# Flamingo layer with routed experts: block tables built with one block per partition, and four pieces of the attention turns in another order

## The reference

```python
# x (8, 256, 256), ctx (8, 120, 256)
qh, kh, vh = x_norm @ Wq, ctx @ Wk, ctx @ Wv   # 16 query heads in 4 groups, 4 key heads of 16
attn = softmax(rope(sum of groups of qh) . rope(kh) / 4)
x = x + tanh(g_xattn) * ((attn @ vh).mean over heads @ Wo)
# experts: 2048 tokens, 8 experts, top 2
probs = softmax(layernorm(x) @ gate_w.T);  w, idx = top_k(probs, 2);  w = w / sum(w)
for e in range(8):
    g, u = split(layernorm(x) @ gate_up_proj[e].T)
    acc += combine[:, e] * (silu(g) * u @ down_proj[e].T)
x = x + tanh(g_ffn) * acc
```

## Time and profile before

| | us |
|---|---|
| median of 3 runs | 457.68 |
| lowest and highest | 455.27, 459.23 |
| the profiled execution | 455.51 |
| its span, first to last instruction | 453.7 |

### The profile page before, as it was taken

The page is one execution under the profiler, slowest core; times in us unless marked ns, Lnnn a source line. Parts: engine busy times, 40 slices in busy tenths (PEclk is TensorE's granted clock), DMA queues, the critical chain, the costliest instruction groups (busy, mean ns, idle before and its releaser), DMA issues.

```text
span 453.7 us, 10877 instructions
## 1 busy us (share of the span) xinstructions
PE 407.9 (90%) x2468; PEld 342.4 (75%) x2469; DVE 220.6 (49%) x589; ACT 204.9 (45%) x453; POOL 258.3 (57%) x257
## 2 busy tenths in 40 slices
PE   7877787666799999999999999999999999999960
PEld 6644464444688888888898888988889888888850
DVE  2566998886334434344443344443444434434330
ACT  2569866221563246336435622563347336433210
POOL 3116879853467239936953972498229936953221
PEclk9999888859699999999999999999999999999975
DMA  8960024821054213531632461146213541112110
GB/s 274 404 249 25 23 97 169 275 73 48 1 175 138 51 24 110 160 102 24 209 117 42 137 192 24 24 116 210 46 24 89 162 122 24 24 24 37 37 28 12
DMA packets 19625, 46.68 MB, mean 103 GB/s; under 512 B 2369, under 2 KB 13761, under 8 KB 16513
## 3 DMA queue, kind: packets, MB, share of 16 engines
q1 hardware_dynamic: 11632, 35.20, 22.4%
q0 software_dynamic: 6720, 9.64, 11.6%
q10 hardware_dynamic: 1248, 1.57, 1.0%
HBM read 37.67 MB, written 9.00 MB: 103 GB/s over the span
## 4 chain that ended last, share of the span: by engine, by line
PE 75%; DVE 9%; DMA 4%; ACT 3%; POOL 3%; issue 3%; POOLq 1%; SPq 0%; DVEq 0%; ACTq 0%
PE att L1010 21%; PE sc L990 20%; PE misc L990 10%; PE qbank L990 10%; PE pT L1000 6%; DMA x<-in_x 2%; POOL dn L472 2%; PE att L974 2%; ACT gu L638 1%; PE att L789 1%; DVE stats L1074 1%; PE sc L827 1%; DMA out<-xT_all,index_out 1%; DVE dn L1201 1%; PE qbank L814 1%
## 5 line engine op out<-in xcount | busy, mean ns | idle before, releaser
L530 POOL DMA_INDIRECT out<-xT_all,index_out x34 | 54.5, 1604 | 111.8 <-DVE xT_all L1421 97.2
L1010 PE MATMUL att<-dn,hT 128*128 x816 | 115.8, 292 | 0.6 <-DVE hT L1399 0.6
L1010 PEld LDWEIGHTS att<-dn,hT 128*128 128x128 f32 x816 | 103.0, 192 | 1.0 <-issue 0.9
L990 PE MATMUL sc<-gu,xT 128*128 x408 | 102.4, 400 | 0.0
L990 PEld LDWEIGHTS sc<-gu,xT 128*128 128x128 f32 x408 | 74.1, 188 | 14.7
L990 PE MATMUL misc<-gu,xT 128*128 x204 | 81.5, 400 | 1.5 <-ACT xT L711 0.9
L990 PE MATMUL qbank<-gu,xT 128*128 x204 | 81.6, 400 | 0.0
L397 POOL TENSOR_TENSOR gu<-wraw,gu 128x2048 f32 x14 | 64.4, 4614 | 12.8 <-ACT gu L627 12.0
L1395 DVE TENSOR_TENSOR xT_all<-xT_all,sc 128x512 f32<-128x512 f32 x34 | 23.4, 688 | 87.6 <-ACT xT_all L718 87.6
L718 ACT ACTIVATE xT_all<-misc 128x512 f32<-128x512 f32 x34 | 20.3, 598 | 81.0 <-PE qbank L990 74.8
L1395 DVE TENSOR_TENSOR xT_all<-xT_all,qbank 128x512 f32<-128x512 f32 x34 | 23.4, 688 | 62.7 <-ACT xT_all L718 62.7
(11 more groups left out here) (169 smaller groups left out, 482.8 us busy)
## 6 DMA issues: line engine op xcount, KB each, us to landing
wraw<-in_gu SPq DMA_DIRECT2D x16, 1024.0 KB, 5.4
wraw<-in_dn SPq DMA_DIRECT2D x8, 1024.0 KB, 5.2
x<-in_x SPq DMA_DIRECT2D x8, 266.0 KB, 11.7
xT_all<-in_xT SPq DMA_DIRECT2D x4, 512.0 KB, 11.3
out<-x SPq DMA_DIRECT2D x8, 256.0 KB, 2.2
rows_scratch<-x SPq DMA_DIRECT2D x3, 532.0 KB, 3.9
xT_all<-rows_scratch,index_in POOLq DMA_INDIRECT x37, 2.9
out<-xT_all,index_out POOLq DMA_INDIRECT x34, 3.9
```

Of the source, the lines that this page charges most:

```text
L530: nc.gpsimd.indirect_dma_start(out=out_d, out_offset=bass.IndirectOffsetOnAxis(ap=index, axis=0), in_=y[:, r, :], in_offset=None, compute_ ...
L990: mm = nc.tensor.matmul(bank[2 * hf + n][:, :], xT[:, par, xp, k, :], gu_part(where, wp, k * 2 * I + col, HALF), start=(k == 0 and xp == 0 ...
L1010: mm = nc.tensor.matmul(bank[6][:, 0:D], hT[:, hf, hp, j * P:(j + 1) * P], dn_part(where, wp, (hf * JH + j) * D, D), start=(hf == 0 and j ...
```

## The change

**The tables.** Block s now stands on partition s. Two columns of constants, `row` (the partition's number) and `row_above` (one less), take the place of the row `blocks`. Fifteen operations of 8 elements a partition (the sum has 32) make five columns `tab_rows`; PE multiplies each column with the identity, which lays the five out as 5 x 44 numbers on partition 0 of the bank `misc`; one DVE copy writes `tab`. There is one semaphore for all readers, `tables_ready`, and POOL's second to sixth gathers and PE's step 0 wait for it. `aside` is a helper for an operation that nothing right behind it needs. PE now warms with one matmul ahead of the five small ones and one behind them.

```diff
             pe.wait_ge(pT_copied, TB * B)
-            stay_warm(3)
+            stay_warm(1)
+            pe.wait_ge(rows_tabled, 1)
+            for k in range(5):
+                mm = nc.tensor.matmul(tab_ps[:, k * NCOL:(k + 1) * NCOL], tab_rows[:, k:k + 1], ident[:, 0:NCOL],
+                                      start=True, stop=True)
+            mm.then_inc(tab_psum, 1)
+            stay_warm(1)
             transpose_x(0)
-            pe.wait_ge(experts_ready, 1)
+            pe.wait_ge(tables_ready, 1)
             step(0, 0, first=True)
```

```diff
             find_tokens()
-            link(V.tensor_tensor(by_block, for_blocks(endblk[:, :]), all_blocks, ALU.is_le))
-            link(V.tensor_reduce(tabf[:, 0, :], by_block, AX.X, ALU.add))
...
+            aside(V.tensor_scalar(by_row[:, 0, :], endblk[:, :], c("row"), None, ALU.is_le))
+            aside(V.scalar_tensor_tensor(out=by_row[:, 1, :], in0=endblk[:, :], scalar=c("row"), in1=skip[:, :],
+                                         op0=ALU.is_le, op1=ALU.mult))
...
+            link(V.tensor_reduce(row_sum[:, :], by_row[:, :, :], AX.X, ALU.add))
...
+            dve.sem_inc(rows_tabled, 1)
+            dve.wait_ge(tab_psum, 1)
+            V.tensor_copy(tab[0:1, :, :], tab_ps.rearrange("o (k s) -> o k s", k=5)).then_inc(tables_ready, 1)
             x_low(0, 0)
-            link(V.tensor_tensor(by_base, by_block, for_blocks(skip[:, :]), ALU.mult))
...
-            V.tensor_tensor(tab[:, 2, :], tabf[:, 1, :], tabf[:, 2, :], ALU.add).then_inc(tables_ready, 1)
```

```diff
-                elif t + 3 < B:
-                    first_moments(t + 3)
-                if ranked is not None:
-                    for b in SETS[ranked]:
-                        mark_slots(b)
                 if t >= 1:
                     best_two(t - 1)
...
+                if ranked is not None:
+                    for b in SETS[ranked]:
+                        mark_slots(b)
                 if t >= 1:
                     second_moments(t - 1)
+                    if t + 3 < B:
+                        first_moments(t + 3)
```

```diff
                 if t < B:
                     copy_pT(t, 0)
-                if t - 2 in ENDS:
-                    second_odds(ENDS[t - 2])
...
                 if t + 1 < B:
                     exponentials(t + 1, 0)
                     exponentials(t + 1, 1)
+                if t - 2 in ENDS:
+                    second_odds(ENDS[t - 2])
```

```diff
                 elif t - 2 in ENDS:
-                    share_out(ENDS[t - 2])
                     place_values(ENDS[t - 2])
                     for b in SETS[ENDS[t - 2]]:
                         mark_places(b, PICKS)
+                    share_out(ENDS[t - 2])
```

More of the change, by code:

```diff
@@ L86, in _const_columns @@
     for name, n in (("ident", P), ("kcos", A), ("ksin", A), ("rope", S), ("before", P), ("prio", E),
-                    ("base", E), ("limits", E * NT), ("upto_it", E * E), ("blocks", NCOL),
+                    ("base", E), ("limits", E * NT), ("upto_it", E * E), ("row", 1), ("row_above", 1),
                     ("first", E), ("alone", E), ("second", E), ("place", P), ("begin", BEGINS), ("token", NT),
@@ L206, in build_program @@
         assert at + (DEPTH - 1) * PICKS * P <= 2 * DN
-        at = E * NT + 2 * NCOL * E
-        at += 2 * NCOL * E
+        at = E * NT
         from_begin = area[:, at:at + BEGINS]
-        assert at + BEGINS <= KC * B * A and PICKS * P <= 2 * NCOL * E
+        assert at + BEGINS <= KC * B * A
         late = xT_all[:, :, :].rearrange("p k n -> p (k n)")
@@ L1357, in _ @@
-            link(V.tensor_tensor(first_by[:, :, :], first_by[:, :, :], over(skip[:, :], FIRSTS), ALU.mult))
-            link(V.tensor_reduce(first_f[:, :], first_by[:, :, :], AX.X, ALU.add))
-            V.tensor_tensor(first_tab[:, :], first_f[:, :], c("blocks")[:, 0:FIRSTS], ALU.add).then_inc(firsts_ready, 1)
-            link(V.tensor_tensor(by_block, for_blocks(endblk[:, :]), all_blocks, ALU.is_le))
-            link(V.tensor_reduce(tabf[:, 0, :], by_block, AX.X, ALU.add))
-            link(V.tensor_scalar(tab[:, 0, :], tabf[:, 0, :], float(E - 1), None, ALU.min))
@@ L1377, in _ @@
-            link(V.scalar_tensor_tensor(out=piece_code[:, 0, :], in0=nblk[:, :], scalar=1.0, in1=c("alone"),
-                                        op0=ALU.is_equal, op1=ALU.mult))
-            link(V.tensor_tensor(piece_code[:, 0, :], piece_code[:, 0, :], c("first"), ALU.add))
-            link(V.tensor_copy(piece_code[:, 1, :], c("second")))
-            for n in range(2):
-                link(V.tensor_tensor(by_piece[:, n, :, :], for_blocks(piece_at[:, n, :]), all_blocks, ALU.is_equal))
-                link(V.tensor_tensor(by_piece[:, n, :, :], by_piece[:, n, :, :], for_blocks(piece_code[:, n, :]),
-                                     ALU.mult))
@@ new lines, in _ @@
+            aside(V.scalar_tensor_tensor(out=by_row[:, 1, :], in0=endblk[:, :], scalar=c("row"), in1=skip[:, :],
+                                         op0=ALU.is_le, op1=ALU.mult))
+            aside(V.tensor_tensor(startblk[:, :], endblk[:, :], nblk[:, :], ALU.subtract))
+            aside(V.scalar_tensor_tensor(out=code_second[:, :], in0=nblk[:, :], scalar=1.0, in1=c("second"),
+                                         op0=ALU.is_gt, op1=ALU.mult))
+            link(V.scalar_tensor_tensor(out=code_first[:, :], in0=nblk[:, :], scalar=1.0, in1=c("alone"),
+                                        op0=ALU.is_equal, op1=ALU.mult))
@@ new lines, in _ @@
+            aside(V.tensor_scalar(tab_rows[:, 3:4], endblk[:, E - 1:E], c("row"), None, ALU.is_gt))
+            aside(V.scalar_tensor_tensor(out=by_row[:, 3, :], in0=startblk[:, :], scalar=c("row_above"), in1=code_second[:, :],
+                                         op0=ALU.is_equal, op1=ALU.mult))
+            link(V.tensor_tensor(code_first[:, :], code_first[:, :], c("first"), ALU.add))
+            link(V.scalar_tensor_tensor(out=by_row[:, 2, :], in0=startblk[:, :], scalar=c("row"), in1=code_first[:, :],
+                                        op0=ALU.is_equal, op1=ALU.mult))
@@ new lines, in _ @@
+            link(V.tensor_reduce(row_sum[:, :], by_row[:, :, :], AX.X, ALU.add))
+            aside(V.tensor_scalar(tab_rows[:, 0:1], row_sum[:, 0:1], float(E - 1), None, ALU.min))
+            aside(V.scalar_tensor_tensor(out=tab_rows[:, 4:5], in0=row_sum[:, 1:2], scalar=c("row"), in1=tab_rows[:, 3:4],
+                                         op0=ALU.add, op1=ALU.mult))
+            aside(V.tensor_copy(tab_rows[:, 1:2], row_sum[:, 3:4]))
+            aside(V.tensor_scalar(last_block[:, :], endblk[:, E - 1:E], -1.0, None, ALU.add))
@@ L1477, in shape_constants @@
     put("upto_it", (np.arange(E)[None, :] <= np.arange(E)[:, None]).reshape(1, E * E))
-    put("blocks", np.arange(NCOL)[None, :])
+    put("row", np.arange(P)[:, None])
+    put("row_above", np.arange(P)[:, None] - 1)
     put("place", np.arange(P)[None, :])
```

59 lines of the change are left out of this document (17 added, 42 removed).

## The result

| | before | after |
|---|---|---|
| median | 456.21 us | 453.48 us |
| lowest, highest of 20 runs | 453.19, 459.29 | 451.12, 455.77 |
| the profiled execution | 455.51 us | 451.98 us |
| its span | 453.7 us | 450.2 us |

What follows compares the result with a forecast made beforehand. PE was taken to bound the expert blocks, so gains lay ahead of the loop and in PE's clock. 455.51 - 2.7 (wait) - 2.65 + 2.4 (clock) + 0.75 (turns) = 453.3 profiled, median 455.5; range 451.5 to 460.

Steps and rivals of the forecast that it cites:

- The wait: PE ahead of the loop: the idle 2.41 us goes, plus 0.3 of the next 0.61; gain 2.7 us.
- The second gather: POOL's second gather waits for the whole table; its stage comes near 108.4, covered by 1 us, so no cost.
- The clock behind the idle time: Loop's first matmuls and the transposes no longer run at the low clock behind PE's idle stretch; gain 2.65 us.
- The clock in step 0: With less warming, step 0's first twelve matmuls run at the low clock; cost 2.4 us, bounds 0 and 4.8.
- The turns: Reordered work in the turns: 1.25 us lost in turn 7, 0.5 won in turn 5; 0.75 us later in sum.
- Turn 5: DVE's comparisons move mostly out of the time of POOL's splits; 0.5 us won, between 1.9 won and 0.9 lost.
- The slower rival: Turns 3, 5 and 7 plus low clock lose more than the tables win; 4.0 us slower, 461.7; chance 0.12.
- signs of being right: No ACT table wait, no PE idle over 1 us before the loop, tables' copy near 104, first group 5 us.
- sign of being wrong: token_at later than 102.5 or sooner than 99.5, a stage-bound second transpose, full clock throughout step 0, or new low loop stretch.

Runs made afterwards that it cites:

- warm_two: The changed kernel with two warming matmuls instead of one ahead of the wait for the table columns; 452.23 us, ratio 0.9897 to before.
- tables_warm2: New tables, turns as before, two warming matmuls instead of one ahead of the columns; 451.71 us, ratio 0.9876 to before; repeated: 450.67 us, 0.9880.
- tables_moments_odds: New tables, turns as before except first_moments at the end of a turn and second_odds behind the exponentials; 452.99 us, ratio 0.9908 to before.
- turns_only: The kernel before with only the four edits in the turns, old tables kept; 457.69 us, ratio 1.0025 to before.
- tables_marks_late: New tables, turns as before except mark_slots moved behind the choice and the logit gap; 452.47 us, ratio 0.9897 to before.
- after_again: The changed kernel itself, unmodified, timed once more beside other variants; 453.85 us, ratio 0.9925 to before.
- tables_only: The changed kernel with its four edits in the turns undone; 451.32 us, ratio 0.9893 to before; repeated: 451.78 us, 0.9920.

## Why the prediction was right, and where it was not

The medians differ by 2.7 us where I had 2.2, and the two profiled executions by 3.5. The mechanism of the tables and of the clock held; that of the turns did not, though its sum came out near. Term by term:

**The wait.** The step held, its size was a little too small. From the start of step 0 to the loop the four traces with full clock there (`warm_two`, `tables_warm2`, its repetition and `tables_moments_odds`) take 6.19 to 6.69 us; before took 9.79, with full clock up to its idle stretch. That is 3.1 to 3.6, where I had 2.7. Of the missing part 0.3 is in the 0.61 us of idle time ahead of the loop's first matmul, of which I took half, as the entry to the loop. It was all wait: PE now has no idle time there, so the wait was 2.41 + 0.61 = 3.0. The rest is the transposes ahead of it, 0.78 us at the low clock and 0.60 now; they start 0.35 us ahead of the loop's first matmul (115.12 to 115.47), where it was 1.39. I had put 0.25 for them under the clock. The tables came in 3.35 us behind `token_at`, against my 3.8, and ACT waits for no table:

```profile
ACT xT_all L706 <- PE qbank L978: 1.9, 1, 1.9
```

This single wait stands in place of the 6.2 us of the earlier trace rows, and it is for PE. The five small matmuls took 0.89 at the low clock; I had 1.1, and up to 2.2.

**The second gather.** Forecast near 108.4, found at 109.81: the tables came 0.7 us later than forecast, behind the later `token_at`, and between them and POOL's copy lie 1.0 us where I had 0.2. It still cost nothing in this trace, since PE transposes these rows behind the first half, which the low clock had made longer. In `tables_warm2`, where that half was at full clock, PE waited 0.32 us for this stage. The cover of 1 us was used up.

**The clock behind the idle time.** 2.65 forecast. The loop's first step takes 12.29 us before and 9.56 to 9.58 in all twelve traces with the new tables: 2.7 less. Right. (From the loop to the end it is 337.24 against 334.45 to 335.40, 1.8 to 2.8 less; there the end of the kernel adds its own spread.)

**The clock in step 0.** 2.4 forecast for a first half that is all low, bounds 0 and 4.8. The change paid 7.71 - 6.25 = 1.5 in one trace and 2.5 in the other; of the eight traces with one warming matmul one had the full clock by itself (`tables_moments_odds`, 6.19), the seven others paid 1.5 to 2.5. All three traces with two matmuls there and none further ahead had it full. So with one matmul 1 trace of 8 and with two 3 of 3 have the full clock from step 0's start. The mechanism is shown in kind; which of its ends an execution meets varies. I had quoted the Trainium skill's page "TensorE: Matmul & The Clock Gate" ("Part 1: The HAM clock gate") for a place of the transition that varies from run to run, with no row to bear it out; the two traces of one program, 7.71 and 8.72, now do.

**The turns.** The sum of 0.75 lies near the 1.1 us of `turns_only` [-0.4, 2.6], but its reason was wrong, and so this part of the forecast was right by luck. I wrote that in turn 7 nothing takes the place of the comparisons, and charged 1.25 us for DVE. The idle time came (1.70 us, as forecast), and yet in the trace of after it isn't what ends last. DVE and POOL in turns 7 and 8:

```profile
83.63 0.25 DVE L1132 MAX8 top<-att 128x8 f32<-128x8 f32 x2 [1.70 <-PE att L856]
...
86.71 1.37 DVE L1195 TENSOR_TENSOR dn<-const,slot_f 128x552 fp32r<-128x552 f32 x2
...
93.61 0.16 DVE L1220 SCALAR_TENSOR_TENSOR x<-mv,x 128x2 f32<-128x2 f32 x1 [1.29 <-POOL x L409]
93.69 0.73 DVE L1195 TENSOR_TENSOR dn<-const,slot_f 128x552 fp32r<-128x552 f32 x1
...
97.02 0.16 DVE L1220 SCALAR_TENSOR_TENSOR x<-mv,x 128x2 f32<-128x2 f32 x1 [0.70 <-POOL x L409]
```
```profile
84.39 7.42 POOL L467 TENSOR_SCALAR dn<-const,slot_f,value 128x128 fp32r<-128x128 f32 x8
91.78 0.29 POOL L445 TENSOR_TENSOR route<-route,odds 128x64 f32<-128x64 f32 x1
92.15 0.28 POOL L449 TENSOR_TENSOR x<-route 128x32 f32<-128x32 f32 x1
92.52 0.23 POOL L407 TENSOR_SCALAR vareps<-mv 128x2 f32<-128x2 f32 x1
92.84 0.73 POOL L409 TENSOR_TENSOR x<-vareps,expo 128x2 f32<-128x2 f32 x1
```

DVE waits for POOL's inverse deviation (L409), which stands behind eight marks that now take 0.85 us more and behind `share_out` (0.7 us), that used to stand ahead. I had called POOL's marks "needed by PE turns later, so nothing" and had given `share_out` no word. What I had not asked is what is queued behind them on POOL. It could be read in the kernel before, in its chain of waits for 84 to 97 us:

```profile
85.25 6.57 POOL dn L472 x8
91.82 0.08 issue
91.91 0.23 POOL vareps L412
...
92.23 0.73 POOL x L414
```

POOL is the chain in those turns, from 85.25 on, so what lengthens or moves its marks there is paid. I had read the chain for the whole span, where POOL has 3%. In the traces in which PE's clock is low for longer in turns 6 and 7 `best_two` comes 2 to 4 us later and DVE doesn't wait for POOL the first time. There the edits cost 0.5 to 0.75 for the one comparison that moved behind the last MAX8 (9.63 against 8.9 to 9.1, which is its 0.65), and another 0.5 with all edits together. Most of this 0.5 is the second wait for POOL's inverse deviation: 0.70 us in all five traces with three or four of the edits, 0.33 in `tables_marks_late`. In these five the whole comparison lies beside the first of POOL's two last marks, which takes 1.25 to 1.32 us instead of 0.81. Which edit brings the two together I can't say.

**Turn 5.** The half microsecond forecast as won can't be seen. The comparisons fell from 3.25 to 2.61 us, about as expected, but `best_two` of turn 6 starts at 76.0 to 77.9 with the old turns and at 76.1 to 79.1 with the new. In `tables_moments_odds` the comparisons take 1.37 us in turn 5 too, since POOL's four splits begin behind them there (70.68 against 69.25), and this gains nothing either: `best_two` of turn 6 starts at 76.18.

**The slower rival** had the right kind of price (turns against tables), but it needed over 5.4 us of turns and clock together. By the traces the turns cost 1 to 2.6 and the clock 1.5 to 2.5.

**The signs.** In the first trace all signs of being right are there, but the group of step 0's first matmuls takes 4.5 us, not 5. In `after_again`, the same program, one sign of being wrong is there too: `token_at` starts at 102.52, later than 102.5, behind a wait of 3.99 us for PE in turn 7. It doesn't count against the mechanism, since traces with the turns of before reach 102.4 as well, but it shows that a bound taken from a single trace was too narrow.

## What to carry to other kernels

Before an instruction is moved to a time in which "its engine has room", look at what other engines run there, and read the chain of waits for that stretch, not for the span: here 1.4 us of DVE work, moved out of an idle hole of DVE and beside POOL's marks, slowed POOL by 0.85 us against before, just where POOL was the chain. By these traces, warming PE is worth its matmuls directly ahead of dense work, and gave nothing where another engine set the time.

## What the runs showed that I had not expected

The same program up to `token_at`, in the four traces of `tables_only` and `tables_warm2` and their repetitions, reaches it at 98.54 to 102.36 us. The spread of 3.8 us goes with PE's clock: over 72 to 88 us the mean granted clock is 1.00 and 0.89 in the two early ones and 0.61 in the two late ones. It is larger than the effect of any edit in the turns. A 0.2% effect isn't to be had from medians of 6 to 12 runs in such a kernel, but the stretches between named instructions repeat to 0.1 us as long as PE doesn't bound them (8.88 to 8.96 in five of eight), and they told the edits apart.
